# Attention stage of an eight-part transformer kernel: masks ahead of the transposes, scores behind the values

## The reference

```
qh, kh, vh = 16 heads of width 16 from layernorm(x), ctx, ctx
scores = einsum('bhqd,bhkd->bhqk', qh, kh) / sqrt(16)
scores = where(k <= q, scores, -10000)
attn   = softmax(scores);  out = einsum('bhqk,bhkd->bhqd', attn, vh)
x      = x + tanh(g_xattn[1]) * out
```

## Time and profile before

| what | value |
|---|---|
| median of three runs | 876.32 us |
| profiled execution, its time / its span | 878.24 us / 876.5 us |
| busy: PE, DVE, ACT, POOL | 787.2, 567.0, 315.8, 159.3 us |
| attention stage, about 461 to 600 us | span 139 us |
| PE busy, 488 to 503 us / 588 to 594 us | 14.76 of 15 us / 1.15 of 6 us |

### The profile page before, as it was taken

One profiled execution on the slowest core, in us unless ns is written; L12 is line 12 of the kernel. 1 busy time (PEld: TensorE's weight loads), 2 busy tenths in 40 slices (PEclk: granted clock), 3 DMA queues, 4 the chain that ended last, 5 costly groups with the idle time before them and its releaser, 6 DMA issues.

```text
span 876.5 us, 13441 instructions
## 1 busy us (share of the span) xinstructions
PE 787.2 (90%) x4627; PEld 635.7 (73%) x4627; DVE 567.0 (65%) x1022; ACT 315.8 (36%) x507; POOL 159.3 (18%) x211
## 2 busy tenths in 40 slices
PE   3887887799999999999997999967599999999994
PEld 2675776689888888888884545536588878888884
DVE  4787778444664564467446888882446785867764
ACT  2120211223423433343244777746143423324221
POOL 2977877200000000031000212121010000000000
PEclk9999999999999999999998999995589999999997
DMA  7221321000000000001001121200000000000000
GB/s 276 73 90 49 103 67 30 1 1 1 1 0 0 0 0 0 0 1 38 12 1 49 55 87 54 86 1 13 1 1 1 1 24 0 0 24 0 24 1 25
DMA packets 22134, 26.09 MB, mean 30 GB/s; under 512 B 5328, under 2 KB 17744, under 8 KB 21968
## 3 DMA queue, kind: packets, MB, share of 16 engines
q1 hardware_dynamic: 22096, 25.60, 9.0%
HBM read 23.22 MB, written 2.10 MB: 29 GB/s over the span
## 4 chain that ended last, share of the span: by engine, by line
PE 67%; DVE 16%; issue 7%; POOL 4%; ACT 3%; SPq 1%; DMA 1%; DVEq 0%; POOLq 0%; ACTq 0%
PE bank L1589 21%; PE bank L1457 19%; PE bank L1470 11%; PE bank L1520 2%; POOL A L459 2%; PE bank L1510 2%; DVE small L1071 2%; PE bank L1598 2%; DVE A L874 2%; DVE A L1081 1%; PE bank L1530 1%; DVE A L863 1%; ACT A L653 1%; POOL R L450 1%; PE bank L1385 1%
## 5 line engine op out<-in xcount | busy, mean ns | idle before, releaser
L1589 PE MATMUL bank<-R 128*128 128x512 f32 (+3 forms) x1080 | 214.5, 359 | 11.2 <-DVE R L1235 4.9
L1589 PEld LDWEIGHTS bank<-R 128*128 128x128 f32 (+1 forms) x1080 | 181.0, 190 | 44.2 <-DVE R L1235 5.1
L1457 PE MATMUL bank<-R 128*128 128x512 f32 x768 | 186.2, 392 | 1.9 <-issue 1.9
L1457 PEld LDWEIGHTS bank<-R 128*128 128x128 f32 x768 | 140.3, 188 | 29.4 <-issue 2.1
L1019 DVE TENSOR_TENSOR A<-bank,A 128x512 f32<-128x512 f32 (+1 forms) x68 | 47.1, 692 | 113.9 <-PE bank L1457 111.6
L1470 PEld LDWEIGHTS bank<-R 128*128 128x128 f32 (+1 forms) x816 | 105.8, 190 | 10.5 <-issue 4.1
L1470 PE MATMUL bank<-R 128*128 128x256 f32 (+1 forms) x816 | 109.4, 283 | 2.5 <-DVE R L1029 2.2
L595 ACT ACTIVATE A<-bank 128x512 f32<-128x512 f32 (+1 forms) x68 | 40.7, 599 | 189.1 <-PE bank L1457 181.5
L874 DVE TENSOR_TENSOR A<-bank,A 128x512 f32<-128x512 f32 x64 | 43.8, 684 | 20.0 <-PE bank L1375 15.2
L1520 PEld LDWEIGHTS bank<-ident,A 128*128 128x128 f32 x256 | 29.0, 146 | 34.7 <-ACT A L653 26.9
L1373 PE MATMUL bank<-A 128*128 128x256 f32 x128 | 40.9, 402 | 14.7 <-DVE A L874 13.5
(11 more groups left out here) (163 smaller groups left out, 1046.7 us busy)
## 6 DMA issues: line engine op xcount, KB each, us to landing
A<-in_w SPq DMA_DIRECT2D x16, 384.0 KB, 3.2
A<-in_w SPq DMA_DIRECT2D x8, 480.0 KB, 3.4
A<-in_ctx_one SPq DMA_DIRECT2D x8, 272.0 KB, 3.5
A<-in_ctx_half SPq DMA_DIRECT2D x8, 256.0 KB, 3.5
A<-in_ctx_nat SPq DMA_DIRECT2D x4, 512.0 KB, 5.2
A<-in_ctx_t SPq DMA_DIRECT2D x128, 16.0 KB, 2.0
out<-X SPq DMA_DIRECT2D x4, 512.0 KB, 2.9
A<-in_filt SPq DMA_DIRECT2D x1, 1536.0 KB, 11.6
```

The lines of the kernel that those rows point to most:

```text
L1457: mm = nc.tensor.matmul(dst[0:pr], wX[:, j, at + k * P:at + k * P + pr], mX[:, k], start=(n == 0), stop=(n == 5))
L1589: mm = nc.tensor.matmul(dst, a, m, start=start and n == 0, stop=stop and n == len(prods) - 1, skip_group_check=skip)
```

## The change

The two mask matmuls leave `c_scores` and become `c_masks`, with the wait on `shifted`. In pass k TensorE before ran S(k+2) with its masks first (not in pass 0), then Q, P(k+1), O(k-1), V(k). It now runs O(k-1), Q, M(k+3), P(k+1), V(k), S(k+3). Nothing is added or taken away on any engine, and the lists of the other engines stay as they are. One wait ahead of Q is gone, since O, with the same wait, now stands ahead of it.

```diff
-            def c_scores(g, k):
+            def c_masks(g, k):
                 n = 8 * g + k
-                r, b, kk = k // 4, k // 2, k % 2
-                pe.wait_ge(qT_ready, BG * g + b + 1)
-                pe.wait_ge(kbd_loaded[r], 16 * 2 * HH * (g + 1))
                 if not (isinstance(n, int) and n < 2):
                     pe.wait_ge(shifted, n - 1)
                 for c in range(2):
                     nc.tensor.matmul(S_[k % 2][:, c * 512:(c + 1) * 512], identb[:], neg[:], start=True, stop=False)
+
+            def c_scores(g, k):
+                r, b, kk = k // 4, k // 2, k % 2
+                pe.wait_ge(qT_ready, BG * g + b + 1)
+                pe.wait_ge(kbd_loaded[r], 16 * 2 * HH * (g + 1))
                 for c in range(2):
...
                 for k in range(8):
-                    if k and (k < 6 or more):
-                        c_scores(g + (k + 2) // 8, (k + 2) % 8)
-                    if more and k in TURN_AT:
-                        pe.wait_ge(ot_taken, 8 * g + k)
-                        c_turn_q(g + 1, TURN_AT.index(k))
-                    if k < 7 or more:
-                        c_turn_p(g + (k + 1) // 8, (k + 1) % 8)
                     if k:
                         c_turn_o(g, k - 1)
                     if more and k in TURN_AT:
+                        c_turn_q(g + 1, TURN_AT.index(k))
+                    if k < 5 or more:
+                        c_masks(g + (k + 3) // 8, (k + 3) % 8)
+                    if k < 7 or more:
+                        c_turn_p(g + (k + 1) // 8, (k + 1) % 8)
+                    if more and k in TURN_AT:
                         pe.wait_ge(qT_ready, BG * (g + 1) + TURN_AT.index(k) + 1)
                     c_values(g, k)
-                if more:
-                    c_scores(g + 1, 2)
+                    if k < 5 or more:
+                        c_scores(g + (k + 3) // 8, (k + 3) % 8)
...
-            c_scores(0, 0)
-            c_scores(0, 1)
+            for k in range(2):
+                c_masks(0, k)
+                c_scores(0, k)
             pe.wait_ge(qT_ready, BG)
             c_turn_p(0, 0)
+            c_masks(0, 2)
             c_scores(0, 2)
```

## The result

The changed kernel takes 870.0 us (median of 13 runs, 868.29 to 875.7) against 876.32 (13 runs), a ratio of 0.9931 with a 95% interval of 0.991 to 0.9952: by the ratio 6.0 us less, 4.2 to 7.9 (the two medians lie 6.3 apart). Forecast were 4.0 us and 872.3. The profiled execution took 869.0 us against 878.24. Of these 9.2 us, 5.7 lie in the attention stage: from its first P to the first transpose for the next stage 127.78 us against 133.46.

What follows compares the result with a forecast made beforehand. The prediction took a TensorE-to-exponential latency loop, 7.39 us per two passes, to bind the attention loop; terms for looped groups and ends summed to -4.02 us, moving the median from 876.32 to 872.3 us, range 869.3 to 875.5.

Steps and rivals of the forecast that it cites:

- Part 1: Attention loop: the maximum starts 1.67 us after P's end, 0.76 earlier, so the latency loop binds no more.
- Part 3: TensorE's runs in new places: prices assumed unchanged in sum, a pass staying 3.40 us, 3.62 with Q.
- Part 2: Masks M(k+3) wait for shift k+1 ahead of P(k+1); done before P could start, otherwise up to 0.54 us a pass.
- the sentence on O: O behind S finds its input copied: ScalarE finishes 2.43 us after P's start, S ends at 2.71.
- third rival: New neighbours cost half: one exposed load of 0.22 us a pass on TensorE, total 874.6 us; chance 0.12.
- the rival with one break less: TensorE's pass 3.29 us, 3.51 with Q, as masks save a break between matmul kinds; total 871.5 us; chance 0.15.
- Part 4: GpSimd holds VectorE's addition in pass 1 of each group, eating what passes 2 to 4 would gain.
- the fixed 9.99: Time in us from pass 1's exponential to the end of P of pass 4, the same before and after.
- the term of 0.44: Last group: the last maximum waited 0.44 us for S, which now comes 0.54 earlier, so -0.44.
- The rival that the clamp slips: Last group: line 1075's clamp slips ahead of GpSimd, saving 1.65 us more, total 870.6 us; chance 0.15.
- The sign that spoke against it: Last group: clamp expected at +2.09 us, GpSimd at +2.03, so the difference had the wrong sign by 0.06.
- The half clock: Slow stretch behind 594 us: either edge could move by some microseconds in either sign; chance 0.05.

Runs made afterwards that it cites:

- e2_masks_only: Changed kernel with O back between P and V, so only masks and scores move (Q M P O V S); ratio 0.9931 to the kernel before.
- e1_o_only: Only O moves against the kernel before; masks stay right ahead of their scores (O Q P V M S); ratio 0.9987 to the kernel before.
- e6_after_last_high3: Changed kernel with ScalarE's first `c_high` of the last group in pass 3 instead of 1; ratio 0.9925 to the kernel before.
- e7_after_lasto_high3: Changed kernel with the last group's first `c_high` in pass 3 and O between P and V in that group; ratio 0.9937 to the kernel before.
- e4_high_2_6: Changed kernel with `c_high` of the looped groups in passes 2 and 6 instead of 1 and 5; 866.37 us, ratio 0.9866 to the kernel before.
- e3_last_o_between: Changed kernel with O between P and V, as before the change, in the last group alone; ratio 0.9941 to the kernel before.
- e5_before_last_high3: Kernel before the change, with the last group's first `c_high` in pass 3 instead of 1; ratio 0.9998 to the kernel before.

## Why the prediction was right, step by step

The direction was right, the range held the time, and two thirds of the measured 6.0 us were in the sum. What was missing are two rivals that were given 0.15 each, and both came true together; the prediction put that case at 869.8 us and made the range reach below it, and 870.0 were measured. So the forecast's mechanism is right and its number is short by these two. Term by term, from the profile, in us:

| term | forecast | measured |
|---|---|---|
| pass 4 of the first group, from the stage's start | -0.18 | -0.15 |
| two looped groups, 29.21 forecast | -2.00 | -2.15 |
| on to pass 0 of the last group | -0.51 | -0.67 |
| to the exponential of pass 1 | -0.46 | -0.42 |
| from there to the last P | -0.44 | -1.87 |
| last P to the next stage (V ahead of O) | -0.43 | -0.42 |
| sum | -4.02 | -5.68 |

- *Part 1, the scores come sooner.* Right. From P's end to the maximum it is now 1.67 us or a few hundredths off (478.48 to 480.16 in the first group), and the alternation of 3.50 and 3.94 became 3.50 to 3.54. `e2_masks_only` shows that this and Part 3 carry the loop's gain, `e1_o_only` that the order of O alone is worth a third of it.
- *Part 2, the masks' wait.* Right: no wait of M for the shift appears in the changed kernel's profile, and one of 0.31 us in its repeat, in the last group; where one is long (2.30 us in `e2_masks_only`) P would have waited as long for the exponential. But the sentence on O looked at one of its two waits, the copy by ScalarE. The other, for VectorE's read of the result, holds O and P for 2.29 us in the last group, and O for 0.09 us in pass 7 of the looped groups. `e6_after_last_high3` and `e7_after_lasto_high3` show that it costs nothing in the last group, since VectorE binds.
- *Part 3, the new neighbours.* No change was taken for TensorE's pass; the end at 0.11 less was the true one (3.51 with Q). `e1_o_only`, with the masks between V and S, keeps 3.62, and `e2_masks_only` has 3.51. (The prediction says that by the Trainium skill's rule the sum would be nearer its third rival; the rival with one break less is its second.) By the sum of that rival the groups come to 28.94 instead of 29.21, and 29.12 to 29.15 were measured. The trace says why not 28.94: passes 5 to 7 take 10.73 and not 10.53, since P of pass 7 comes 3.70 behind the one ahead of it. From there the forecast's own path adds up: 10.73+1.67+3.93 to the maximum, 2.81 to the exponential, and the fixed 9.99 make 29.13.
- *Part 4, GpSimd holds VectorE.* Right to 0.01 us, and `e4_high_2_6` shows its price: 0.78 a group.
- *The last group.* The step that came out otherwise is "VectorE with its statistics binds and its order is not touched: 0". The maxima show it, first before, then after:

```profile
578.67 1.22 DVE L1071 TENSOR_REDUCE small<-bank 128x8 f32<-128x1024 f32 x1
...
582.55 1.19 DVE L1071 TENSOR_REDUCE small<-bank 128x8 f32<-128x1024 f32 x1
```

```profile
578.02 1.23 DVE L1071 TENSOR_REDUCE small<-bank 128x8 f32<-128x1024 f32 x1 [0.63 <-PE bank L1512]
...
582.03 1.22 DVE L1071 TENSOR_REDUCE small<-bank 128x8 f32<-128x1024 f32 x1
```

Counted from the exponential of pass 1, the first of three maxima came at 8.42 (578.67) and comes at 6.34 (573.43), 2.08 sooner: the clamp is not held, 1.66, and it starts 0.41 sooner. The second came at 12.30 and comes at 10.93: it now waits 0.63 for its scores, with TensorE at the lower clock, and 0.71 of the 2.08 is lost (in the repeat, at the full clock, it does not wait). The third came at 16.81 (587.06, behind a wait of 0.44) and comes at 14.94 without a wait, 0.50 more: this is the term of 0.44, and it was right. Together -1.87.

The rival that the clamp slips, given 0.15, is thus what the sum lacked. `e3_last_o_between` and `e2_masks_only` show it from one side (held at 0.22 and 0.24 behind GpSimd, 1.4 to 1.7 us longer), `e5_before_last_high3` from the other (free in the old order, 1.67 shorter). The sign that spoke against it, 0.06 us behind GpSimd's start, was not evidence: the earlier trace rows already had a clamp that started in the same hundredth and went free.
- *The half clock.* The 3.1 us of the router run in the profiled execution come from a stretch of higher clock. Such a stretch is also in `e1_o_only`, at 0.59 from 594 to 612 us against 0.50 before, whose time is that of the kernel before within its interval. So it is not counted to the change. The medians differ by 6.3 us and the profiled stages by 5.7, which leaves some 0.6 for it; how often each kernel meets such a stretch was not measured.

## What to carry to other kernels

When a loop is bound by latency between two engines, measure from the end of the producer's last input to the start of the consumer and take out of that stretch what the consumer does not need; here 0.76 us of masks and transposes out of it made two passes 0.4 us shorter, until the next bound, 0.1 us away, took over. Then place the work of an engine that can hold another one by its start time against each instruction it can hold, not by its load: the same move of GpSimd's work gave some 0.6% in the new order (0.9866 against 0.9931 and, in the repeat, 0.992) and cost 0.66% in the old. In both orders it is a matter of hundredths: the clamp is free 0.02 to 0.04 us ahead of GpSimd in the one and held 0.22 to 0.23 behind it in the other. And count every wait of an instruction that is moved, also the ones that were never seen to wait.

## What the runs showed of the hardware

A VectorE clamp of 128x8 elements, 0.17 us long, is held for the rest of a GpSimd instruction of 2.22 us in all eight cases of these profiles in which it starts 0.22 to 0.42 us behind it (2.02 at 0.22, 2.02 at 0.24, 1.82 at 0.42). It is not held if it starts ahead of it or 0.00 to 0.02 behind it (527.16 and 527.16 in the earlier trace rows, 569.13 against 569.11, 568.56 against 568.55). No run has a start between 0.02 and 0.22, so where the border lies is not shown. The 128x256 addition of two SBUF tensors is held as well: wherever it starts 1.28 to 1.90 us behind GpSimd, it ends 0.27 to 0.29 us behind GpSimd's end. Maxima, shifts and products that read PSUM (1.23, 1.22 and 0.48 us) and the statistics (two in 0.75 us) keep their usual time. The Trainium skill (GPSIMD Engine Reference, Specifications) says that GpSimd's SBUF interfaces are shared with VectorE, with contention for instructions in a 2-port mode or with two SBUF inputs; the trace agrees for the addition, and shows that the contention is a wait to the end and not a slower run. The clamp has one SBUF tensor as input; whether it runs in a 2-port mode no run here shows.
